# Routed expert loop of a four-part layer: fetching the gathered rows already turned, as two 16-bit planes

## What is computed

```python
x = x + tanh(g_xattn[0]) * mamba(ctx_1024, layernorm(x), ...)
x = x + tanh(g_ffn[0])   * experts(layernorm(x), ...)
x = x + tanh(g_xattn[1]) * attention(layernorm(x), ctx_1024, ...)
x = x + tanh(g_ffn[1])   * quantised_ffn(x, ...)
```

```python
scores = sigmoid(x @ gate_w)
_, selected = top_k(scores + expert_bias, 2)
comb = scores of the selected two, divided by their sum        # zero for other experts
shared = (silu(x @ shared_gate_w) * (x @ shared_up_w)) @ shared_down_w
for e in range(16):
    g, u = split(x @ experts_gate_up[e])                       # 512 -> 256 and 256
    routed = routed + comb[:, e] * ((silu(g) * u) @ experts_down[e])
return shared + routed
```

## Time and profile before

| | us |
|---|---|
| median of 3 runs | 1567.27 |
| lowest and highest | 1563.79, 1568.78 |
| the profiled execution | 1568.37 |
| its span | 1566.5 |
| TensorE busy | 1450.0 (93%) |
| VectorE busy | 1110.2 (71%) |
| ScalarE busy | 967.5 (62%) |
| GpSimd busy | 633.0 (40%) |
| first and last matmul of L1357 (up product) start | 570.5, 868.4 |

### The profile page before, as it was taken

The page is one execution under the profiler, slowest core; times in us unless marked ns, Lnnn a source line. Parts: engine busy times, 40 slices in busy tenths (PEclk is TensorE's granted clock), DMA queues, the critical chain, the costliest instruction groups (busy, mean ns, idle before and its releaser), DMA issues. The chain is left out here.

```text
span 1566.5 us, 21482 instructions
## 1 busy us (share of the span) xinstructions
PE 1450.0 (93%) x6233; PEld 632.0 (40%) x6245; DVE 1110.2 (71%) x1628; ACT 967.5 (62%) x1544; POOL 633.0 (40%) x410
## 2 busy tenths in 40 slices
PE   6688988989988999999999998799999999999999
PEld 2334434434444444444444444133333333244444
DVE  7999999999995422222222488898999999647985
ACT  3999999999964011111111244477788788877764
POOL 0689799698971630064646556104000000000000
PEclk7799999989999999999999999699999999999999
DMA  5212314113214485357832655352322322130465
GB/s 188 68 51 84 94 53 122 41 55 115 68 30 181 156 221 174 121 188 251 285 121 92 200 192 162 94 188 74 94 76 73 95 74 77 56 108 14 88 140 122
DMA packets 137914, 183.45 MB, mean 117 GB/s; under 512 B 55491, under 2 KB 83523, under 8 KB 136819
## 3 DMA queue, kind: packets, MB, share of 16 engines
q1 hardware_dynamic: 114518, 128.29, 28.6%
q0 software_dynamic: 8416, 29.43, 6.0%
q10 hardware_dynamic: 14912, 24.89, 4.8%
HBM read 109.29 MB, written 54.92 MB: 105 GB/s over the span
## 5 line engine op out<-in xcount | busy, mean ns | idle before, releaser
L1918 DVE TENSOR_REDUCE a_mx<-a_s 128x2 f32<-128x1024 f32 x256 | 303.3, 1218 | 37.7 <-PE a_s L2035 34.9
L283 POOL TENSOR_TENSOR m_hs<-m_hs,m_C 128x1024 f32<-128x1024 f32 x128 | 301.8, 2383 | 54.6 <-DVE m_hs L508 53.9
L508 DVE TENSOR_TENSOR_SCAN m_hs<-m_dA,m_d 128x512 f32<-128x512 f32 x256 | 294.7, 1201 | 11.6 <-PE m_d L663 10.1
L663 PE MATMUL m_d<-ident_sb,m_dBuT 128*128 128x128 f32 x1024 | 160.5, 291 | 16.9 <-DVE m_hs L508 9.9
L663 PEld LDWEIGHTS m_d<-ident_sb,m_dBuT 128*128 128x128 f32 x1024 | 117.9, 146 | 142.2 <-DVE m_hs L508 71.7
L389 ACT ACTIVATE m_dA<-m_dt,m_negA 128x512 f32<-128x512 f32 x256 | 167.8, 711 | 10.7 <-DMA m_dt<-m_dt 9.9
L1357 PE MATMUL e_gu<-e_w,e_xgT 128*128 x376 | 169.1, 592 | 0.0
L2035 PE MATMUL a_s<-ring_sb 96*128 96x512 bf16 x512 | 153.0, 391 | 7.7 <-DVE a_mx L1918 4.1
L367 ACT ACTIVATE m_dBuT<-m_dtuT,m_BT 128x512 f32<-128x512 f32 x241 | 157.8, 711 | 0.5 <-PE m_d L663 0.3
L678 PE MATMUL m_y<-m_hs,m_fold 128*64 128x512 f32 x512 | 142.3, 636 | 3.1 <-POOL m_hs L283 3.1
L1007 ACT ACTIVATE e_sg<-e_gu 128x256 f32<-128x256 f32 x47 | 18.0, 384 | 194.7 <-PE e_gu L1357 194.7
(11 more groups left out here) (347 smaller groups left out, 2462.3 us busy)
## 6 DMA issues: line engine op xcount, KB each, us to landing
e_w<-in_ex_gu SPq DMA_DIRECT2D x16, 1024.0 KB, 6.2
ring_sb<-qk_dram SPq DMA_DIRECT2D x64, 192.0 KB, 3.1
xg_dram<-zeros_sb SPq DMA_DIRECT2D x47, 256.0 KB, 3.1
e_xg<-xg_dram ACTq DMA_DIRECT2D x47, 256.0 KB, 2.8
yg_dram<-attn_sb ACTq DMA_DIRECT2D x47, 256.0 KB, 2.0
m_C<-c_dram SPq DMA_DIRECT2D x64, 128.0 KB, 2.9
m_dt<-m_dt SPq DMA_DIRECT2D x64, 128.0 KB, 2.4
e_w<-in_ex_dn SPq DMA_DIRECT2D x16, 512.0 KB, 7.7
```

What stands on the lines that cost most here:

```text
L283: pool.tensor_tensor(hs[:, J % RH], hs[:, J % RH], C2[:, N % RC].unsqueeze(1).broadcast_to([P, 2, L]), ALU.mult).then_inc(s_hc, 1)
L508: dve.tensor_tensor_scan(hs[:, J % RH, h], dA[:, j % RA], pd[j % RD][:], 0.0, ALU.mult, ALU.add)\
L663: last = pe.transpose(pd[j % RD][:, t * P:(t + 1) * P], dBuT[:, N % 2, t, g], ident[:])
L1918: dve.tensor_reduce(mx[:, r % 2, h * TB + 2 * c:h * TB + 2 * c + 2], psc[c][:], AX.X, ALU.max)\
```

## The change

Each row is kept in `xg_dram` as two planes of 512 16-bit numbers, first the low halves of its 512 numbers and then the high halves. GpSimd makes the planes before the scatter, with one `tensor_copy` of 128x1024 16-bit numbers per tile of tokens. The planes of tile t take the place of the normalised rows of tile t-1, once TensorE has turned those; the first take `xgT[:, 0]`. The load of a tile becomes one transposing DMA of ScalarE, from 128 rows of 1024 16-bit numbers to 8 blocks of 128x128, the low halves in the first four. In place of the copy from PSUM, ScalarE writes the two planes interleaved into `xgT` (here "the join"), 1024 16-bit numbers per partition; no arithmetic changes a bit. Before it issues the load of tile j+2 it now waits for the end of this join, which reads the buffer that the load writes. TensorE's `fetch` is gone with its waits. The zeroing and the scatter are the same bytes named as 16-bit numbers. ScalarE's two loops on the device become straight code, with fixed addresses and wait values.

```diff
@@ mamba, zeroing
-                                 zeros[:].unsqueeze(1).broadcast_to([P, 2, D // 2])).then_inc(s_zero, 16)
+                                 zeros[:].bitcast(U16).unsqueeze(1).broadcast_to([P, 2, D])).then_inc(s_zero, 16)
@@ moe, buffers
-        xg = sb("xg", [P, 2, D])
+        xp = sb("xp", [P, 2, 2 * KD, P], U16)
         xgT = sb("xgT", [P, 2, KD, P])
+        planes = [xgT[:, 0].rearrange("p k t -> p (k t)")] + [xn[:, t] for t in range(NT - 1)]
+        s_pl = sem("rows_in_halves")
@@ moe, GpSimd
+            for t in range(NT):
+                pool.wait_ge(s_xn, t + 1)
+                if t >= 1:
+                    pool.wait_ge(s_xt, t)
+                    pool.wait_ge(s_pl, t)
+                pool.tensor_copy(planes[t].bitcast(U16).rearrange("p (h d) -> p h d", h=2),
+                                 xn[:, t].bitcast(U16).rearrange("p (d h) -> p h d", h=2)).then_inc(s_pl, 1)
+            pool.wait_ge(s_pl, NT)
             pool.wait_ge(s_slot, 1)
             pool.wait_ge(s_zero, 16 * ST)
             for k in range(2):
                 for t in range(NT):
                     pool.indirect_dma_start(xg_dram.rearrange("j p d -> (j p) d"),
                                             bass.IndirectOffsetOnAxis(ap=slot[:, k, t:t + 1], axis=0),
-                                            xn[:, t, :], None).then_inc(s_sct, 16)
+                                            planes[t].bitcast(U16), None).then_inc(s_sct, 16)
@@ moe, ScalarE
             def load(j, par):
-                act.dma_start(xg[:, par], xg_dram[bass.ds(j, 1)].rearrange("o p d -> (o p) d"))\
-                    .then_inc(s_ld[par], 16)
+                act.dma_start_transpose(xp[:, par], xg_dram[j]).then_inc(s_ld[par], 16)
             def tile(j, par, more=True):
-                act.wait_ge(s_xt, NT + 1 + j)
+                act.wait_ge(s_ld[par], 16 * (j // 2 + 1))
                 act.wait_ge(s_gu, NB + j - 1)
-                act.activation(xgT[:, par], pxt[par][:], ACT.Copy).then_inc(s_xtc, 1)
+                act.activation(xgT[:, par].bitcast(U16).rearrange("p k (t h) -> p h k t", h=2),
+                               xp[:, par].rearrange("p (h k) t -> p h k t", h=2), ACT.Copy).then_inc(s_xtc, 1)
                 if more:
+                    act.wait_ge(s_xtc, NT + j + 1)
                     load(j + 2, par)
-            with act.Fori(0, KEYS_FROM) as i:
-                pair(i)
-            with act.Fori(0, B) as b:
-                for f in range(KD):
-                    pair(b * KD + (f + KEYS_FROM))
-                    copy_key(b, f)
-            for i in range(KEYS_FROM + KD * B, (ST - 5) // 2):
-                pair(i)
+            for i in range((ST - 5) // 2):
+                pair(i)
+                if 0 <= i - KEYS_FROM < KD * B:
+                    copy_key(*divmod(i - KEYS_FROM, KD))
@@ moe, TensorE
-            def fetch(j, par, nload):
-                pe.wait_ge(s_ld[par], nload)
-                if not (isinstance(j, int) and j < 2):
-                    pe.wait_ge(s_xtc, NT + j - 1)
-                for k in range(KD):
-                    last = pe.transpose(pxt[par][:, k], xg[:, par, k * P:(k + 1) * P], ident[:])
-                last.then_inc(s_xt, 1)
                 turn(i * 2 + (m - 1), (m - 1) % 2)
                 routed_up(i * 2 + m, m % 2, e)
-                if not last:
-                    fetch(i * 2 + (m + 1), (m + 1) % 2, (i + (m + 1) // 2) * 16 + 16)
                 routed_down(i * 2 + (m - 1), (m - 1) % 2, before)
@@ build
-    xg_dram = dram("xg_dram", (ST, P, D))
+    xg_dram = dram("xg_dram", (ST, P, 2 * D), U16)
```

More of the change, by code:

```diff
@@ L1438, in pair @@
                 e2 = expert(i * 2 + 2)
-                step(i, 2, e1, e2, last)
-            fetch(0, 0, 16)
+                step(i, 2, e1, e2)
             shared_down(NT - 2)
@@ L1463, in _ @@
                 pair(i)
-            pair((ST - 1) // 2 - 1, last=True)
+            pair((ST - 1) // 2 - 1)
             e = expert(ST - 1)
```

8 lines of the change are left out of this document (4 added, 4 removed).

## The result

The changed kernel takes 1582.4 us in the median (1566.1 to 1586.3) against 1565.9 for the kernel before beside it: a ratio of 1.0078, interval 1.0054 to 1.0103. It is slower by 0.8%, where 1.1% faster was forecast. The same kernel, run again with 12 executions, gave 1580.1 (1566.0 to 1585.9), ratio 1.0073 (1.0047 to 1.0099). The execution with the profile took 1566.1, one of its best. The page of the kernel after: its span, the busy time of the engines, the packets of ScalarE's queue, and two groups of instructions.

What follows compares the result with a forecast made beforehand. TensorE was taken to bound the routed loop, busy 299.90 of 300.90 us. 20.2 - 1.5 (join) - 1.0 (start) = 17.7 us saved, giving 1550.7 by the profiled execution, hence 1549.6 us; range 1546 to 1562.

Steps and rivals of the forecast that it cites:

- The turns: TensorE in the routed loop: 188 turns of fetched rows go, 47 tiles by 0.43 us, 20.2 us saved.
- (a) The silu chain: Up, silu, product, turn in each tile: just covered without the fetched rows' turns, so no cost.
- its old pace: Rival: the silu chain has no reserve, 0.2 to 0.43 us per tile is taken back, 1558 to 1567; chance 0.08.
- (b) The join: ScalarE behind the silu: join taken as 1.05 us, 0.05 late for 30 of 46 up products, 1.5 us in all.
- my own rule: Join on ScalarE: from 1.05 us upward each 0.1 us costs 30 x 0.1 = 3 us.
- (c) The load in quiet stretches: Transposing load on ScalarE's queue: lands in 3 to 5 us against a budget of 9.6, issue 0.75 to 1.5; hidden.
- (d) The start: First loads of the loop, beside tables and 4 MB of later weights: 1 us booked.
- That rival: Small packets wait their turn at the start: a load takes 17.5 us, TensorE loses 8 us once, 1557.6; chance 0.15.
- (e) The plane copies: GpSimd ahead of the scatter: 16 copies of 1.04 us, 18 us in all, done at 506; hidden with 11 us to spare.
- the bound that I had set for it: Scatter on GpSimd: the prediction is wrong if it starts later than 518 us.
- (f) Straight code: Unrolled ScalarE loops, 2-byte zeroing and scatter, fixed addresses: zero, bounds 0 and 1 us; GpSimd's 11.9 us idle covers the keys.
- neither the join nor the loads are a bound: Slower rivals for the loop: join at 2.1 us, 1581, chance 0.06; loads at 10.8 us each, about 1775, chance 0.04.

Runs made afterwards that it cites:

- typical execution: The profiled execution (1579.4 us) of the unaltered changed kernel's second run; that run's median was 1580.1 us, ratio 1.0073 to the kernel before.
- e4_join_first: Changed kernel with tables and the 4 MB spread over the first eight down products, and ScalarE's join ahead of the silu: 1559.5 us, ratio 0.9951 to the kernel before.
- e5_first_alone: Changed kernel with only ScalarE's order changed, join ahead of silu, tables and 4 MB as in the change: 1572.3 us, ratio 1.0021 to the kernel before.
- e3_both_spread: Changed kernel with one piece of the 4 MB and one table behind each of the first eight down products: 1567.9 us, ratio 1.0008 to the kernel before.
- e1_before_cut: Kernel before with only 64 columns of the 4 MB loaded and the tables after the eighth tile: 1575.2 us, ratio 1.0051 to the unaltered one.

## Why the prediction was wrong

*The turns* (20.2 us): right. The distances reach 5.37 as soon as the join is off the path, 0.44 less than 5.81.

*(a) The silu chain*: right. At 5.37 it is just covered, and TensorE does not keep its old pace.

*(b) The join*: the mechanism was right, the size was not. 1.34 us against 1.05 is 0.29 more, and by my own rule (3 us for each 0.1) that takes 8.8 of the 18.7 us that turns and join came to. For the 42 distances behind the start, taken as 42 of 46, that is 8.0 of 17.1; measured are 11.1, so 6.0 were lost. The nearest row wrote its 16-bit numbers contiguously. I noted the interleaving as an upper bound and then took the value of the row that lacked it. I also priced the join only as late; that it could stand ahead of the silu, and the whole bill then goes, I did not see.

*(c) The load in quiet stretches*: right. It lands in 3.0 us at the least and 3.7 in the median, and its issue takes 1.25. Instructions of the transposing load and their landing in the kernel after, and landing in its typical execution, answer to the earlier trace rows:

```profile
L1063 ACTq DMA_TRANSPOSE e_xp<-xg_dram x47: 1247/1249/6407, 561.3 to 856.6; - x47
...
DMA to landing us min/median/max: 3.0/3.7/19.3
```

```profile
DMA to landing us min/median/max: 3.1/3.9/34.5
```

The Trainium skill, VectorE: DVE Perf Modes, "The three transpose paths", gives 1309 ns for one 128x128 block, and eight of them in a row would have made the time near 1760, an estimate. The trace disagrees with that reading: eight blocks landed in 3.0 us are under 0.4 us a block.

*(d) The start*: this is the step that failed. I booked 1 us and gave 8 us a chance of 0.15; it is 14 to 25. That rival named what came, loads in small packets that land late beside a neighbour's large ones, and its size fell short for three reasons. First, I read the price where the first loads do not run. From 587 to 589 us, beside the 4 MB, each engine started one of ScalarE's packets every 0.27 us; a packet of GpSimd's took 0.14 us there (73.7% of 32 us in 163). The first loads run beside the tables. The queues of the kernel before from 564 to 578 us:

```profile
DMA packets 382, 1.85 MB, mean 132 GB/s; under 512 B 119, under 2 KB 119, under 8 KB 169
...
q0 software_dynamic: 332, 1.75, 95.6%
q10 hardware_dynamic: 50, 0.10, 6.2%
```

95.6% of 14 x 16 = 224 us in 332 packets are 0.645 us each in the mean; 119 of them are tiny, and the 213 of 8 KB take about 1 us. If each of 65 packets waited for one of that mean, a load would take 42 us, not 17.5, as an estimate; the longest landing in the typical execution is 34.5. The worst plain load, 10.8 us, was issued at 568.98, in this very stretch, and I had not asked where it stood. Second, I let one load be late; in the first execution four were (14.3, 16.7, 19.3 and 10.7 us), in the typical one three (18.5, 34.5 and 27.3), and each late one delays the issue of the next but one. Third, I took the neighbour's traffic as given. It is slowed too: the typical execution of the kernel after, 580 to 592 us,

```profile
DMA packets 1130, 1.43 MB, mean 119 GB/s; under 512 B 949, under 2 KB 949, under 8 KB 1018
...
q10 hardware_dynamic: 912, 0.23, 75.1%
q0 software_dynamic: 218, 1.20, 68.4%
```

moved 1.43 MB, with q0's packets still 0.60 us long (68.4% of 192 us in 218), so the tables are not yet through: the last landed at 587.9, against 579.3 in the kernel before. In the kernel before, in the same 12 us,

```profile
q0 software_dynamic: 790, 3.98, 82.8%
```

q0 is at the 4 MB already and moves 3.98 MB. The crowd lasts longer, and so does the loss. The falling clock comes on top.

How the engines share themselves out between the queues stays open. One packet for one it is not: in the 12 us above 912 of ScalarE's went beside 218 of GpSimd's. The Trainium skill, DMA: Bandwidth & Descriptors, "Queues, rings and completion order", has an engine go round the queues and take from each a packet of typically 9 to 17 descriptors; whether that is what these rows count, no run here shows. Nor did a run part the two things that the change gave the loads at once, small packets and the transposition: plain loads in packets of 256 bytes were not tried. Shown is that with the traffic taken away the loss at the start goes, and that plain loads beside the same traffic cost TensorE next to nothing (23.39 us for the four distances, 0.15 over the pace).

*(e) The plane copies*: right, 1.04 us each with 0.16 between, done at 504.9. The scatter starts at 518.6, 1.2 us later than before and 0.6 past the bound that I had set for it. That is the spread between executions: it starts at 516.6 in the typical execution, and at 516.4 to 520.2 in those of the kernels with plain loads. The first up product came at 570.7 and 568.7.

*(f) Straight code, the same bytes under other names*: nothing of it shows. GpSimd's 11.9 us of idle time, which I took as cover for the keys, were not: about 2 us of them are to spare, and the shorter loop of e4_join_first lost 2.1 us there. A loop at the pace of the forecast would meet the same; that is an estimate.

So 17.7 us were forecast; 6.0 of them went to the join, and the first four tiles, which were to gain 0.6 (1.6 less 1.0), lost 13.6 to 25.5. With the loss of the typical execution that makes 17.7 - 6.0 - 0.6 - 25.5 = -14.4, where the medians say 13.4 slower. The range was too narrow by leaving the start's far end at 8 us, and the side "slower" had the wrong mechanisms: neither the join nor the loads are a bound throughout, the crowd at the start is what made the kernel slower.

## What to carry to other kernels

A transfer that is cut into many small packets can be free in a quiet stretch and late in a crowded one: price each stretch in which it runs by the packets that share its engines there, and look for the longest of them. More buffers or another issuing engine did not mend that here; thinning the neighbour out did, as far as its pieces did not meet the next crowd. Idle time of an engine ahead of a barrier is not slack until one has looked at what it still has to do there. And a step that takes an operation off the bounding engine should come with the order of the engine that takes it over: here the join cost 0.2 to 0.3 us a tile behind the silu and nothing ahead of it.

## What the runs showed of the hardware

- The issue of a transposing load of 256 KB holds the issuing queue 1.25 us in quiet, where I had expected 0.75 to 1.5, and up to 15.1 in a crowd (e5_first_alone). A plain store issued behind one was held 7.6 us (e3_both_spread). With plain loads alone no issue of ScalarE's took over 0.6 us in a crowd.
- The same load lands after 3.0 us in quiet and up to 35.1 beside the tables and the 4 MB (e5_first_alone); the plain load of the same bytes after 2.4 in quiet, 10.8 beside the tables and 18.1 beside tables and expert weights (e1_before_cut).
- ScalarE's copy of 1024 16-bit numbers takes 1.05 us contiguous, 1.16 when it reads from two places in turn, 1.35 when it writes every other one.
- Loads of 256 KB broadcast to 16 partitions (the tables) move packets of 8 KB in about 1 us each, 0.645 us with the tiny ones between them. Eight in a burst beside expert weights stop even a plain load: TensorE waited 7.27 us for it.
- At the end of a stage GpSimd drains for 5.7 to 6.0 us once its last stores have landed (before, e4_join_first), and the next stage waits for that.
